# One pair of reciprocal-root operations on GpSimd for two samples, and the copy of rows ahead of the wait for their addresses

## What is computed

```
h = layernorm(x)
x = x + layernorm(attention(h, 16 heads, causal) @ w_out + b_out)     # attention layer 0
f = layernorm(x)
for l in 0, 1:                                                       # attention layers 1 and 2
    f = f + attention(ln(f) * ln1_w + ln1_b, with biases)
    g = ln(f) * ln2_w + ln2_b
    l == 0: each token goes to its best 2 of 8 experts (128 -> 512 -> 128, gelu)
    l == 1: each sample of 256 tokens goes to its best 2 of 8 experts
    f = f + weighted sum of the 2 experts
x = x + layernorm(f)
```

## Time and profile before

| | us |
|---|---|
| median of 3 runs | 1150.66 (1150.61 to 1152.04) |
| the profiled execution | 1157.45 |
| its span, first to last instruction | 1155.7 |
| PE (TensorE) busy | 1016.3 (88%) |
| DVE (VectorE) busy | 874.4 (76%) |
| ACT (ScalarE) busy | 774.1 (67%) |
| POOL (GpSimd) busy | 704.8 (61%) |

### The profile page before, as it was taken

How to read it: one execution, slowest core, us unless ns; L and a number is a source line. 1 busy time by engine, 2 the same in 40 slices (tenths; PEclk the granted TensorE clock), 3 DMA queues, 4 the chain that set the end, 5 groups by cost and what they waited for, 6 DMA issues and landing times.

```text
span 1155.7 us, 34934 instructions
## 1 busy us (share of the span) xinstructions
PE 1016.3 (88%) x10453; PEld 790.6 (68%) x10453; DVE 874.4 (76%) x2668; ACT 774.1 (67%) x1913; POOL 704.8 (61%) x1051
## 2 busy tenths in 40 slices
PE   1799999999999999998279999189998999989996
PEld 1567676667777666666179999156666666669986
DVE  3689999999998888887645555178898888856665
ACT  1577777777777777776067778157777777755554
POOL 3456666666767888887723332667887887433331
PEclk9999999999999999999589999689999999999999
DMA  5343222221212222221122222244322222100000
GB/s 153 100 116 82 53 56 53 54 54 51 57 52 61 65 66 65 67 66 42 50 63 72 67 69 64 66 121 129 91 69 66 67 64 60 43 2 15 20 19 23
DMA packets 120711, 73.73 MB, mean 64 GB/s; under 512 B 10736, under 2 KB 115568, under 8 KB 120560
## 3 DMA queue, kind: packets, MB, share of 16 engines
q1 hardware_dynamic: 101552, 51.59, 16.5%
q10 hardware_dynamic: 14912, 11.88, 3.7%
q0 software_dynamic: 4096, 8.40, 2.6%
HBM read 21.68 MB, written 11.60 MB: 29 GB/s over the span
## 4 chain that ended last, share of the span: by engine, by line
PE 31%; DVE 6%; issue 6%; DMA 3%; POOL 3%; ACT 2%; SPq 1%; POOLq 0%; DVEq 0%; ACTq 0%
PE bank L1220 10%; PE bank L1209 9%; PE bank L348 2%; DVE wide L616 2%; DMA stack<-mT 2%; PE bank L393 1%; POOL y_got L944 1%; PE bank L315 1%; PE bank L334 1%; DVE f_all L795 1%; PE bank L1281 1%; PE bank L311 1%; PE bank L375 1%; PE bank L381 1%; ACT prob L503 1%
## 5 line engine op out<-in xcount | busy, mean ns | idle before, releaser
L616 DVE TENSOR_REDUCE wide<-bank 128x2 f32<-128x512 f32 (+1 forms) x576 | 388.6, 678 | 87.2 <-PE bank L307 67.1
L503 ACT ACTIVATE prob<-bank 128x512 f32<-128x512 f32 x576 | 337.0, 592 | 87.2 <-PE bank L329 59.2
L900 POOL TENSOR_SCALAR_AFFINE_SELECT prob<-prob 128x512 f32<-128x512 f32 x384 | 245.9, 647 | 94.9 <-ACT prob L503 92.8
L348 PE MATMUL bank<-prob,vaug 128*32 128x256 f32 (+1 forms) x3072 | 165.9, 334 | 4.7 <-issue 3.4
L1240 POOL COPY w_job<-w_s 128x512 f32 x104 | 65.6, 632 | 155.5 <-PE bank L1209 154.9
L315 PE MATMUL bank<-stack 126*128 126x256 bf16 x768 | 148.7, 274 | 0.0
L334 PE MATMUL bank<-stack 128*128 128x256 bf16 x768 | 147.2, 272 | 0.9 <-ACT prob L503 0.9
L1220 PE MATMUL bank<-w_job,prob 128*128 128x128 f32 x1088 | 138.9, 276 | 1.9 <-issue 1.6
L1231 ACT ACTIVATE prob<-bank,b_job 128x128 f32<-128x128 f32 (+1 forms) x416 | 131.8, 400 | 10.1 <-PE bank L1209 6.9
L348 PEld LDWEIGHTS bank<-prob,vaug 128*32 128x32 f32 x3072 | 81.6, 109 | 78.7 <-issue 46.8
L1220 PEld LDWEIGHTS bank<-w_job,prob 128*128 128x128 f32 x1088 | 131.4, 192 | 5.3 <-issue 4.2
(11 more groups left out here) (185 smaller groups left out, 2032.9 us busy)
## 6 DMA issues: line engine op xcount, KB each, us to landing
stack<-parts SPq DMA_DIRECT2D x576, 64.0 KB
w_s<-e_w ACTq DMA_DIRECT2D x32, 256.0 KB, 3.0
oT<-x_routed SPq DMA_DIRECT2D x72, 64.0 KB, 1.8
y_routed<-oT SPq DMA_DIRECT2D x36, 128.0 KB, 1.9
stack<-mT SPq DMA_DIRECT2D x192, 4.0 KB
out<-x_all SPq DMA_DIRECT2D x16, 128.0 KB, 1.8
b_all<-e_b ACTq DMA_DIRECT2D x2, 512.0 KB, 7.1
x_routed<-hk,x_at POOLq DMA_INDIRECT x64
```

Of the source, the lines that this page charges most:

```text
L348: m = nc.tensor.matmul(o, w, (prob0, prob1)[kb][:, g % 2, h], start=kb == 0, stop=kb == 1, skip_group_check=True)
L503: nc.scalar.activation(o, s, ACT.Exp, scale=SCALE).then_inc(exp_done, 1)
L616: nc.vector.tensor_reduce(o, s, AX.X, ALU.max, negate=True).then_inc(max_done, 1)
L900: nc.gpsimd.affine_select(out=t, in_=t, compare_op=ALU.is_ge, fill=0.0, base=0, pattern=[[0, HG], [1, P]], channel_multiplier=-1).then_inc ...
```

## The change

In slot 2 GpSimd now waits for both moments, takes both items' roots in one pair of operations on 128 x (2 x 2) values, and then does the slot's two selects. For that pre_mv and post_mv, and pre_r and post_r, lie side by side in one tile each, and power has four columns. Where only one of the two items exists, the pair is done for it alone, also ahead of the selects. Who waited for post_rstd now waits for pre_rstd of item v + 4 (post_ready), for late_rstd at the ends of the runs, or for x_rstd for the norm of stage 0. Second, the copy to hk (pool_keep) stands ahead of the send in slot 3, except at the end of the run. pool_select, pool_send and the lists of the other engines keep their places.

```diff
-        power = sb("power", [P, 2])
+        power = sb("power", [P, 4])
...
-        pre_mv = sb("pre_mv", [P, 2, 2, 2])
-        pre_r = sb("pre_r", [P, 2, 2])
+        pre_post_mv, pre_post_r = sb("pre_post_mv", [P, 2, 2, 2, 2]), sb("pre_post_r", [P, 2, 2, 2])
+        (pre_mv, post_mv), (pre_r, post_r) = ([a[:, :, kind] for kind in range(2)] for a in (pre_post_mv, pre_post_r))
...
+        def post_ready(i):
+
+            nxt4, end = i.v + 4, 3 * B if i.v >= 2 * B else 2 * B
+            if nxt4 < end:
+                return pre_rstd, 2 * nxt4 + 2
+            return late_rstd, 2 * (nxt4 - end + (4 if end == 3 * B else 0)) + 2
...
         def dve_residual_moments(i):
-            need(dve, post_rstd, NRSTD * (i.v - 2) + 2)
+            if i.v >= 2:
+                dve.wait_ge(*post_ready(Item(i.v - 2, i.par, (i.v - 2) // B)))
             dve_moments(post_st, post_mv[:, i.par], res, summed(i))
 
         def dve_normalise(i):
 
-            dve.wait_ge(post_rstd, NRSTD * i.v + (2 if i.phase == 0 else NRSTD))
+            dve.wait_ge(*post_ready(i))
...
-        def pool_rstd(mv, r, s, base, last=1):
+        def pool_rstd(mv, r, s, base):
 
             alone(pool)
-            nc.gpsimd.tensor_scalar(r, mv[:, :, 1], EPS, None, ALU.add).then_inc(s, 1)
+            nc.gpsimd.tensor_scalar(r, mv[..., 1], EPS, None, ALU.add).then_inc(s, 1)
             pool.wait_ge(s, base + 1)
-            nc.gpsimd.tensor_tensor(r, r, power[:], ALU.pow).then_inc(s, last)
+            exponents = power[:, 0:2] if len(r.shape) == 2 else power[:].rearrange("p (a b) -> p a b", a=2)
+            nc.gpsimd.tensor_tensor(r, r, exponents, ALU.pow).then_inc(s, 1)
...
+        def pool_keep(i):
+
+            if i and i.phase == 1:
+                pool.wait_ge(res, NRES * i.v + NRES)
+                need(pool, x_sent[i.par], sent(i) - 16 * 2 * TOP)
+                alone(pool)
+                nc.gpsimd.tensor_copy(hk[:, i.par], hn[:, i.par]).then_inc(hk_sb, 1)
...
             if k == 2 and older:
                 pool.wait_ge(res, summed(older) + 4)
-                pool_rstd(post_mv[:, older.par], post_r[:, older.par], post_rstd, NRSTD * older.v,
-                          1 if older.phase == 0 else NRSTD - 1)
-            if k == 0 and oldest and oldest.phase == 0:
-                pool.wait_ge(res, NRES * oldest.v + 12)
-                pool_rstd(mv2[:, oldest.par], r2[:, oldest.par], post_rstd, NRSTD * oldest.v + 2)
-            if ie:
-                pool_select(ie, ge, 0)
             if k == 2 and nxt2:
                 pool.wait_ge(pre_stats, NPRE * nxt2.v + 4)
                 need(pool, xn_ok, 2 * (nxt2.v - 2) + 2)
+            if k == 2 and nxt2 and older:
+                pool_rstd(pre_post_mv[:, nxt2.par], pre_post_r[:, nxt2.par], pre_rstd, 2 * nxt2.v)
+            elif k == 2 and nxt2:
                 pool_rstd(pre_mv[:, nxt2.par], pre_r[:, nxt2.par], pre_rstd, 2 * nxt2.v)
+            elif k == 2 and older:
+                pool_rstd(post_mv[:, older.par], post_r[:, older.par], late_rstd, post_ready(older)[1] - 2)
+            if k == 0 and oldest and oldest.phase == 0:
+                pool.wait_ge(res, NRES * oldest.v + 12)
+                pool_rstd(mv2[:, oldest.par], r2[:, oldest.par], x_rstd, 2 * oldest.v)
+            if ie:
+                pool_select(ie, ge, 0)
...
+            if k == 3 and nxt2:
+                pool_keep(oldest)
             sending = first if k == 3 else item(step, -5)
             if sending and sending.phase == 1:
                 pool_send(sending, (k + 1) % NG)
-            if k == 3 and oldest and oldest.phase == 1:
-                pool.wait_ge(res, NRES * oldest.v + NRES)
-                need(pool, x_sent[oldest.par], sent(oldest) - 16 * 2 * TOP)
-                alone(pool)
-                nc.gpsimd.tensor_copy(hk[:, oldest.par], hn[:, oldest.par]).then_inc(hk_sb, 1)
+            if k == 3 and not nxt2:
+                pool_keep(oldest)
```

More of the change, by code:

```diff
@@ L32 @@
 SPREAD = 4
-NPRE, NRSTD, NRES, NSPLIT = 4, 4, 14, 3
+NPRE, NRES, NSPLIT = 4, 14, 3
 STACK_DMAS = TERMS
@@ L124, in build @@
         post_st = sb("post_st", [P, 2, 6])
-        post_mv = sb("post_mv", [P, 2, 2, 2])
-        post_r = sb("post_r", [P, 2, 2])
         st2 = sb("st2", [P, 2, 6])
@@ L196, in build @@
         o1_ps, attn_n, o2_ps, onT_sb, o3_ps = sem("o1_ps"), sem("attn_n"), sem("o2_ps"), sem("onT_sb"), sem("o3_ps")
-        res, post_rstd = sem("res"), sem("post_rstd")
+        res, late_rstd, x_rstd = sem("res"), sem("late_rstd"), sem("x_rstd")
         hT_ps, hT_sb, lg_ps, lg_sb = sem("hT_ps"), sem("hT_sb"), sem("lg_ps"), sem("lg_sb")
@@ L711, in dve_f @@
         def dve_f(i):
-            dve.wait_ge(post_rstd, NRSTD * i.v + NRSTD)
+            dve.wait_ge(x_rstd, 2 * i.v + 2)
             dve_normal(tiles(f_all, i), tiles(x_all, i), mv2[:, i.par], r2[:, i.par], res)
@@ L883, in dve_slot @@
             if k == 3 and older and older.phase == 0:
-                need(dve, post_rstd, NRSTD * (older.v - 2) + 4)
+                need(dve, x_rstd, 2 * (older.v - 2) + 2)
                 dve_moments(st2, mv2[:, older.par], res, NRES * older.v + 8)
-        def pool_rstd(mv, r, s, base, last=1):
+        def pool_rstd(mv, r, s, base):
             alone(pool)
-            nc.gpsimd.tensor_scalar(r, mv[:, :, 1], EPS, None, ALU.add).then_inc(s, 1)
+            nc.gpsimd.tensor_scalar(r, mv[..., 1], EPS, None, ALU.add).then_inc(s, 1)
             pool.wait_ge(s, base + 1)
-            nc.gpsimd.tensor_tensor(r, r, power[:], ALU.pow).then_inc(s, last)
+            exponents = power[:, 0:2] if len(r.shape) == 2 else power[:].rearrange("p (a b) -> p a b", a=2)
+            nc.gpsimd.tensor_tensor(r, r, exponents, ALU.pow).then_inc(s, 1)
         def pool_select(i, g, u):
```

## The result

| | before | changed |
|---|---|---|
| median, us | 1150.63 (4 runs) | 1162.93 (4 runs, 1161.95 to 1163.34) |
| ratio | | 1.0103, 95% interval 1.0091 to 1.0115 |
| span of the profiled execution, us | 1155.7 | 1161.6 |
| PE busy, us | 1016.3 | 1023.4 |
| DVE busy, us | 874.4 | 874.8 |

A forecast was written before the change was run, and what follows sets the result against it. TensorE and VectorE were taken to form one ring per step, with room on GpSimd. Terms of 12.4, 0.5 and 4.2 us sum to +17, giving 1167.7 us; 8-in-10 range 1149.5 to 1176.

The forecast's parts named there:

- the likeliest case: The forecast itself for the whole kernel: 17 us slower, 1167.7 us, own range 1159 to 1174, chance 0.45.
- Part 1: GpSimd, each step: one pair removed saves about 1.0 us, off the path since nobody waits for pre_r.
- Part 2: Stage 0 and first 3 steps of stage 1: later pair and selects over att cost 19 x (0.30 + x).
- x: What GpSimd's power on 128x4 takes more than on 128x2 (0.71 us); taken as 0.35 us.
- the port's part: SBUF interfaces shared by GpSimd and VectorE: selects hold up VectorE operations, two att operations taking 1.24 us instead of 0.59.
- (a): Rival, whole kernel: the power costs the same for four columns, x = 0; +3 us, 1153.7; chance 0.17.
- (b): Rival, whole kernel: all of the power's time doubles, x = 0.71; +31 us, 1182; chance 0.06.
- Part 3: Stage 1 steps that send rows: hn later, xn and L398's stall (L400 before) give back; -0.30 + x, 9 steps.
- Part 4: Stage 1, GpSimd: the copy to hk falls into the send's wait, 0.40 us earlier; nothing counted for it.
- Part 5: Stage 2: hn ends 0.72 + x later, slack before TensorE's bank just used up; 0.0 + x, 12 steps.
- Rival (c): Faster: GpSimd, the late engine in stages 1 and 2, comes forward; 6 us won, 1144; chance 0.16.
- Rival (d): The delays end in slack, such as L311's 0.5 us in stage 0; unchanged at 1150.7; chance 0.16.

The follow-up runs named there:

- experiment 3: The changed kernel with the first select of slot 2 moved ahead of the pair: 1158.8 us, ratio 1.0058.
- 8: The changed kernel, with GpSimd in slot 2 waiting for VectorE's att or hn before its two selects: 1176.7 us, ratio 1.0219.
- 5: The changed kernel with VectorE taking pre_mv right behind post_mv, so that the pair can start earlier: 1154.9 us, ratio 1.0027.
- Experiment 4: The changed kernel with the pair's power on 8 columns instead of 4, the added ones unused: 1187.8 us, ratio 1.0324.
- experiment 2: The changed kernel with the copy to hk put back behind the send, so the pair alone: 1163.0 us, ratio 1.0112.
- experiment 7: The kernel before, its two pairs kept separate, with only the first select of slot 2 moved ahead of them: 1149.4 us, ratio 0.9978.
- experiment 6: The changed kernel with both pre_mv right behind post_mv and the first select of slot 2 ahead of the pair: 1156.6 us, ratio 1.0038.

## Why the prediction was right

It said slower by 17 us, 1167.7; measured was slower by 12.3, 1162.93, within the likeliest case's own range (1159 to 1174).

- **Part 1, the removed pair, off the path:** right. GpSimd is 28 us less busy, and its idle time ahead of the pair is put down to the moments.
- **Part 2, stage 0:** the mechanism is right in each step, the term was too large: 12.4 us forecast for its 19 steps, 10.6 measured. att begins 1.58 us after pre_mv's end (0.20 + 1.01 + 0.04 + 0.33), att takes 1.25 us, xn 0.59, L309 is the place. The stall was forecast as 0.40 + x = 0.73 and is 0.70. The step grew by 0.59, that is 0.26 + x, where 0.30 + x was taken between TensorE's 0.40 and VectorE's 0.22. The side of VectorE played no part: TensorE fell back only at L309, by 0.70 less the 0.10 that it had spent just before it, and the 0.22 us that it stood at L400 were those of one odd step. Experiments 3 and 8 show the port's part, 5 that of the start, 4 that of the length.
- **x:** 0.33 for two columns, 0.35 forecast; 4 showed that the per-column price was the right model (0.16 us, I had 0.21 as its upper bound). Rivals (a) and (b) fall by it.
- **Part 3, stage 1:** too small. Forecast for its nine steps was 9 x 0.05 = 0.5 us, measured 1.3, or 0.18 in a steady step. The gain at L398 was forecast as 0.30 and is 0.30, but by luck: the pair alone gives 0.50 there (0.67 to 0.17 in experiment 2), and the copy takes 0.20 of it. xn gives back 0.14 us where 0.30 was forecast. And I had followed hn's 0.40 + x through VectorE alone, and left out that TensorE stands still for it first, at L413 and L309; no run was made for this term by itself.
- **Part 4, the copy:** right that it wins nothing and that the times don't show it. What the part left out is that the copy, too, holds up VectorE: L747 takes 0.38 instead of 0.17 us, which costs 0.07 us in each steady step with sends (experiment 2 against the changed kernel).
- **Part 5, stage 2:** the term that failed most, in size. "There the slack is just used up" gave 12 x 0.35 = 4.2 us; measured 0.8, of which 0.5 in the last of the twelve steps. I let the reduce begin 0.05 us behind hn, while it begins 0.08 before hn's end (872.98 against 871.80 + 1.25). pre_mv ended 0.05 us earlier in the step than before. And of the 0.10 us between the reduce's end and TensorE's load (864.62 and 864.72) 0.05 were slack. Together 0.23 us of x = 0.33 found slack that I had denied, and the remaining 0.10 are how much later L309 comes. Experiment 4 agrees: with that slack used up, 0.63 us more of power cost 0.49 a step.
- **Rival (c), faster,** fell for the reason given: pre_mv ends last before the pair in all three stages. **Rival (d), slack,** was right in the main for stage 2 only.

The misses are 1.8 us too much in part 2, 0.8 too little in part 3 and 3.4 too much in part 5: together the 4.4 us between the sum of 17 and the 12.7 of the steps.

Each of att's operations that met a select took 0.33 us more, and one select less on it took 0.34 us from TensorE's stall (experiment 3). The trace agrees here with the Trainium skill's rule (GPSIMD Engine Reference, Key points) on the shared SBUF interfaces. The power's 0.16 us a column is far from the loop of 2.6 cycles an element that the Trainium skill gives (GPSIMD Engine Reference, Elementwise — side-by-side cycle accounting), and which it measured with an addition. At the 1.2 GHz that this section of the Trainium skill reckons with, 2.6 cycles are 2.2 ns, an estimate; the additions here took 1.7 ns a column, so the agreement that the prediction saw is a rough one.

## What to carry to other kernels

Merging two small operations on an engine that has idle time was worth nothing here, and it ties both results to the later input and to the longer duration: look first for the earliest consumer, and for what was queued behind. An in-order engine that waits is also a schedule: work that stands behind the wait comes out in a block, and if it shares a port with another engine, that block falls on whatever the other engine was waiting to do. Moving such work into the wait (experiment 7) won about 0.2%, which removing 28 us of work (the change) did not. And read more than one step before calling a short wait a cost: the 0.22 us at L400 were one step's.

## What the runs showed of the hardware

- The power on GpSimd costs by the column, even for very few: 0.72, 1.05 and 1.68 us for 2, 4 and 8 columns of float32 on 128 partitions, while the tensor_scalar addition went from 0.229 to 0.230 us from 2 to 4 columns.
- A VectorE tensor_scalar of 128x128 float32 in SBUF takes 0.33 us, and 0.65 to 0.68 when a 0.63 us select of GpSimd has just begun; it ends 0.08 us after the select. Two in a row are held up by two selects in a row, one each. GpSimd's power doesn't hold up the 128x8 operation L623 of the changed kernel (0.17 us in the middle of a power of 1.04 us).
- Which of the two is held up goes by who begins first, in the meetings looked at. In the kernel before x_all begins 0.01 us ahead of a select and takes its usual 0.41 us, and the select takes 0.89 instead of 0.63; in experiment 6 x_all begins 0.05 us behind a select and takes 0.87:

```profile
215.48 0.89 POOL L900 TENSOR_SCALAR_AFFINE_SELECT prob<-prob 128x512 f32<-128x512 f32 x1
```

```profile
215.47 0.41 DVE L709 TENSOR_TENSOR x_all<-x_all,att 128x256 f32<-128x256 f32 x1
```

- GpSimd's copy and addition hold up VectorE too: the 128x4 cast L747 takes 0.38 us beside the copy and 0.17 without it, the 128x8 operation L625 0.53 beside the addition and 0.86 beside addition and copy.
